# Route weights of a mixture of experts: from matmul spreading to DMA copies out of one partition each

## The reference, cut to what matters

```
probs = softmax(flat @ router_w.T)                 # 8 experts
tp, ti = top_k(probs, 2);  tp = tp / (sum(tp) + 1e-9)
weights = sum(tp[..., None] * one_hot(ti, 8), axis=1)
for e in range(8):
    hh = silu(flat @ w1[e].T) * (flat @ w3[e].T)   # 170 hidden features
    out = out + weights[:, e:e + 1] * (hh @ w2[e].T)
return layernorm(h + x + out)
```

## Time and profile before

| | |
|---|---|
| median of 3 runs | 124.4 us (123.87 to 124.7) |
| the profiled execution, its own time | 124.77 us |
| its span in the profile | 122.6 us |
| PE, DVE, ACT, POOL busy | 90%, 69%, 51%, 17% |
| granted TensorE clock over the span | 0.996 |

### The profile page before, as it was taken

How to read it: one execution, slowest core, us unless ns; L and a number is a source line. 1 busy time by engine, 2 the same in 40 slices (tenths; PEclk the granted TensorE clock), 3 DMA queues, 4 the chain that set the end, 5 groups by cost and what they waited for, 6 DMA issues and landing times.

```text
span 122.6 us, 2299 instructions
## 1 busy us (share of the span) xinstructions
PE 110.0 (90%) x890; PEld 72.7 (59%) x890; DVE 84.3 (69%) x181; ACT 62.8 (51%) x123; POOL 20.7 (17%) x46
## 2 busy tenths in 40 slices
PE   5978988899999999999599999799999999999920
PEld 2335537377776764877287888577888866232510
DVE  0001416697999597569887763469689997998981
ACT  4004466865332257635686348567476656247340
POOL 7400035000000000000013002154002340048400
PEclk9999999999999999999999999999999999999998
DMA  4999980000000000000000000000000000000003
GB/s 143 392 391 429 421 360 19 0 0 0 5 0 0 0 8 0 3 0 5 0 0 0 0 5 0 0 5 0 0 0 0 0 0 3 0 0 5 0 0 86
DMA packets 2682, 6.99 MB, mean 57 GB/s; under 512 B 1264, under 2 KB 1392, under 8 KB 2544
## 3 DMA queue, kind: packets, MB, share of 16 engines
q1 hardware_dynamic: 2128, 6.72, 13.9%
q10 hardware_dynamic: 544, 0.13, 0.5%
HBM read 6.59 MB, written 0.26 MB: 56 GB/s over the span
## 4 chain that ended last, share of the span: by engine, by line
PE 59%; DVE 19%; ACT 6%; DMA 5%; issue 4%; POOL 2%; SPq 1%; ACTq 0%; DVEq 0%
PE PS L649 7%; PE PS L650 7%; DMA shared_x<-x_dram 5%; PE PS L657 4%; PE PS L318 3%; PE PS L328 3%; PE PS L534 3%; PE PS L520 3%; PE PS L382 3%; DVE top L1137 2%; DVE shifted L1139 2%; PE PS L392 2%; PE PS L357 2%; PE PS L368 2%; PE PS L293 2%
## 5 line engine op out<-in xcount | busy, mean ns | idle before, releaser
L649 PE MATMUL PS<-xf,up_hi 128*128 128x512 f32 x44 | 17.8, 404 | 0.0
L650 PE MATMUL PS<-xf,up_lo 128*128 128x512 f32 x44 | 17.3, 394 | 0.0
L1331 DVE TENSOR_TENSOR shared_h<-PS,shared_f 128x512 f32<-128x512 f32 x22 | 14.9, 683 | 2.7 <-ACT shared_f L909 2.2
L909 ACT ACTIVATE shared_f<-PS 128x512 f32<-128x512 f32 x22 | 13.0, 596 | 6.3 <-PE PS L650 6.3
L1137 DVE TENSOR_REDUCE top<-PS 128x8 f32<-128x512 f32 x12 | 8.3, 688 | 3.7 <-PE PS L357 1.8
L649 PEld LDWEIGHTS PS<-xf,up_hi 128*128 128x128 f32 x44 | 8.3, 188 | 2.2 <-DVE shared_h L1331 0.2
L737 ACT ACT_TABLE_LOAD x7 | 9.0, 1283 | 0.8 <-PEq L1546 0.7
L650 PEld LDWEIGHTS PS<-xf,up_lo 128*128 128x128 f32 x44 | 8.3, 188 | 1.8
L989 POOL TENSOR_TENSOR qf<-shared_f 128x256 f32<-128x256 f32 x2 | 1.5, 728 | 44.1 <-DVE shared_f L1266 44.1
L808 ACT ACTIVATE probs<-PS 128x512 f32<-128x512 f32 x8 | 4.8, 597 | 7.9 <-PE PS L368 7.8
L285 PE MATMUL PS<-idle_bf 128*128 128x512 bf16 (+1 forms) x22 | 7.5, 446 | 1.3 <-POOL idle_bf L946 1.3
(11 more groups left out here) (194 smaller groups left out, 212.6 us busy)
## 6 DMA issues: line engine op xcount, KB each, us to landing
shared_x<-x_dram SPq DMA_DIRECT2D x3, 576.0 KB, 4.3
shared_x<-x_dram SPq DMA_DIRECT2D x3, 512.0 KB, 8.1
up_w<-pack_d_dram SPq DMA_DIRECT2D x1, 1408.0 KB, 12.4
pack_c_sb<-pack_c_dram SPq DMA_DIRECT2D x1, 796.5 KB, 13.2
pack_b_sb<-pack_b_dram SPq DMA_DIRECT2D x1, 455.0 KB, 9.4
down_w<-pack_e_dram SPq DMA_DIRECT2D x1, 352.0 KB, 13.5
pack_a_sb<-pack_a_dram SPq DMA_DIRECT2D x1, 162.0 KB, 6.6
out_dram<-normed SPq DMA_DIRECT2D x2, 64.0 KB, 1.8
```

Of the source, the lines that this page charges most:

```text
L649: mm(up, up_hi[:, at:at + P], moving, start=True, stop=False)
L650: mm(up, up_lo[:, at:at + P], moving, start=False, stop=True).then_inc(sem("up_mm"), 1)
L909: f(gate[:, n % UPBUF, :], PS[:, UP_BANKS[n % UPBUF][0], :], ACT.Silu).then_inc(sem("gated"), 1)
L1331: v.tensor_tensor(hh[:, ch, :, g * HC:(g + 1) * HC], PS[:, UP_BANKS[n % UPBUF][1], :].rearrange("q (s c) -> q s c", s=2), gate[:, n % UPBU ...
```

## The change: what it does

- The fourth of the four copies of the route weights is no longer split: it holds the full fp32 weights, and after PE's turn they are rows 96 to 111 of the PSUM bank (`EXACT_AT` = 96). A new ACT copy takes these 16 rows to a new tile, `route_exact`, ahead of the spread copies.
- SP waits for it and then issues 16 DMAs inside SBUF, each of which repeats one row of `route_exact` (2 KB in one partition) over 64 or 42 partitions: both streams of expert 2, of expert 3, the rests t = 4 and 5 (two experts each), then both streams of experts 4 to 7. Row `96 + 8 s + e` is the source for stream s and expert e.
- PE spreads experts 0 and 1 and rests 0 to 3 only. Six `spread_routes`, two `spread_rests` and six ACT copies go. The order of the down products is then free of spreading.
- POOL, not DVE, multiplies rests 4 and 5 into `hh`, SBUF by SBUF, before its four sums.
- Several semaphores of earlier stages are merged under one name with counts; their order is the same.

```diff
+        route_exact = sb("route_exact", [P, COLS])
+        rest_spread = (shared_f[:, UPBUF * COLS:(UPBUF + 1) * COLS], shared_x[:, (NE + 3) * COLS:(NE + 4) * COLS])
+        def spread_of(e):
+            return up_w[:, e * COLS:(e + 1) * COLS] if e < 5 else shared_x[:, (NE + e - 5) * COLS:(NE + e - 4) * COLS]
...
# SP
+            sp.wait_ge(sem("exact_made"), 1)
+            def send_route(s, e, dst, name):
+                line = EXACT_AT + s * NE + e
+                sp.dma_start(dst, route_exact[line:line + 1, :].unsqueeze(1).to_broadcast([1, dst.shape[0], COLS])).then_inc(sem(name), 16)
+            def send_expert(e):
+                for s in range(2):
+                    send_route(s, e, spread_of(e)[HALF * s:HALF * s + HALF], f"route_sent{min(e, 4 + e // 6 * 2)}")
+            def send_rests(t):
+                for n, e in enumerate(experts_of(t // 2)):
+                    send_route(t % 2, e, rest_spread[t - 4][n * REST:(n + 1) * REST], "rests_sent")
+            send_expert(2)
+            send_expert(3)
+            send_rests(4)
+            send_rests(5)
+            for e in range(4, NE):
+                send_expert(e)
...
# PE
-            spread_rests(3, 3)
+            spread_rests(3, 0)
+            pe.wait_ge(sem("exact_made"), 1)
             expert_down(1, DOWN_BANKS[1], every)
             pe.wait_ge(sem("rest_weighted"), 1)
             expert_down(2, DOWN_BANKS[2], every)
...
+            pe.wait_ge(sem("rest_weighted"), 2)
+            expert_down(3, DOWN_BANKS[3], every)
+            for e in range(4, NE):
+                pe.wait_ge(sem("expert_weighted"), e - 3)
+                expert_down(e, DOWN_BANKS[e], every)
             pe.wait_ge(sem("rest_weighted"), 4)
...
+            pe.wait_ge(sem("last_rests"), 2)
             rests_down(0)
...
# ACT
-            for e in range(NE):
+            f(route_exact[EXACT_AT:EXACT_AT + 2 * NE, :], PS[EXACT_AT:EXACT_AT + 2 * NE, ROUTED_BANK, :], ACT.Copy).then_inc(sem("exact_made"), 1)
+            for e in range(2):
...
# POOL
+            for t in (4, 5):
+                used = REST * len(experts_of(t // 2))
+                pool.wait_ge(sem("rests_sent"), 64)
+                g_.tensor_tensor(hh[0:used, t // 2, t % 2, :], hh[0:used, t // 2, t % 2, :], rest_spread[t - 4][0:used], ALU.mult)\
+                    .then_inc(sem("last_rests"), 1)
...
# DVE
-                ve.wait_ge(sem("routes_out"), e + 1)
+                if e < 2:
+                    ve.wait_ge(sem("routes_out"), e + 1)
+                else:
+                    ve.wait_ge(sem(f"route_sent{min(e, 4 + e // 6 * 2)}"), 32 if e < 4 else 64)
...
-                if e == 1:
-                    weight_rest(4)
-                    weight_rest(5)
```

More of the change, by code:

```diff
@@ L238, in build @@
         DOWN_BANKS = (4, 7, 1, 3, 4, 7, 1, 3)
-        REST_SPREAD_BANKS = (1, 3, 2, 6, 2, 6)
+        REST_SPREAD_BANKS = (1, 3, 2, 6)
+        EXACT_AT = 6 * 2 * NE
         LOGITS_BANK = 4
         ROUTED_BANK = 7
-        SPREAD_BANKS = (0, 5, 0, 5, 2, 6, 2, 6)
+        SPREAD_BANKS = (0, 5)
         FINAL_BANKS = (0, 5)
@@ L670, in spread_routes @@
             def spread_routes(e):
-                rows = slice(4 * NE * (e % 4), 4 * NE * (e % 4 + 1))
+                rows = slice(4 * NE * (e % 3), 4 * NE * (e % 3 + 1))
                 mm(PS[:, SPREAD_BANKS[e], :], pick[rows, e, :], route_rows[rows, :], start=True, stop=True)\
@@ L771, in _ @@
             act.wait_ge(sem("ffn1_down"), 1)
-            f(half(f1, 0), PS[:, FFN1_BANKS[0], 0:HC], ACT.Identity, bias=b("ff2_b")).then_inc(sem("f1_ready0"), 1)
+            f(half(f1, 0), PS[:, FFN1_BANKS[0], 0:HC], ACT.Identity, bias=b("ff2_b")).then_inc(sem("f1_ready"), 1)
             def queries1(g):
@@ L800, in _ @@
             act.wait_ge(sem("ffn1_down"), 2)
-            f(half(f1, 1), PS[:, FFN1_BANKS[1], 0:HC], ACT.Identity, bias=b("ff2_b")).then_inc(sem("f1_ready1"), 1)
+            f(half(f1, 1), PS[:, FFN1_BANKS[1], 0:HC], ACT.Identity, bias=b("ff2_b")).then_inc(sem("f1_ready"), 1)
             scale1 = float(HD) ** -0.5
@@ L1027, in _ @@
             pool.wait_ge(helped, 6)
-            four = routes.unsqueeze(2).to_broadcast([P, 4, 4, 2 * NE])
-            g_.tensor_copy(route_parts[:, :, :, 0, :].bitcast(F32R), four).then_inc(helped, 1)
+            three = routes.unsqueeze(2).to_broadcast([P, 4, 3, 2 * NE])
+            g_.tensor_copy(route_parts[:, :, 0:3, 0, :].bitcast(F32R), three).then_inc(helped, 1)
+            g_.tensor_copy(route_parts[:, :, 3, :, :], routes.unsqueeze(2).to_broadcast([P, 4, 2, 2 * NE])).then_inc(sem("route_split"), 1)
             pool.wait_ge(helped, 7)
-            g_.tensor_tensor(route_parts[:, :, :, 1, :], four, route_parts[:, :, :, 0, :], ALU.subtract).then_inc(sem("route_split"), 1)
+            g_.tensor_tensor(route_parts[:, :, 0:3, 1, :], three, route_parts[:, :, 0:3, 0, :], ALU.subtract).then_inc(sem("route_split"), 1)
+            for t in (4, 5):
[3 more added lines that the diff above has]
+                    .then_inc(sem("last_rests"), 1)
             def sum_pair(dst, other):
@@ L1050, in block_sums @@
             def block_sums(name, w, n):
-                v.reduce_sum(means[:, 0:n], w.rearrange("q (n d) -> q n d", d=D), AX).then_inc(sem(name + "_sum"), 1)
+                v.reduce_sum(means[:, 0:n], w.rearrange("q (n d) -> q n d", d=D), AX).then_inc(sem("block_sums"), 1)
             def less_means(name, w, n):
                 blocks = w.rearrange("q (n d) -> q n d", d=D)
-                ve.wait_ge(sem(name + "_sum"), 1)
+                ve.wait_ge(sem("block_sums"), 1 + ("av", "abv", "down").index(name))
                 return v.scalar_tensor_tensor(out=blocks, in0=means[:, 0:n].unsqueeze(2).to_broadcast([P, n, D]),
@@ L1404, in _ @@
                 ve.wait_ge(sem("down_mm"), e + 1)
-                ve.wait_ge(sem("routes_out"), e + 1)
-                v.tensor_tensor(product[:, e], PS[:, DOWN_BANKS[e], :], spread_w[:, e % 4], ALU.mult)\
+                if e < 2:
+                    ve.wait_ge(sem("routes_out"), e + 1)
+                else:
+                    ve.wait_ge(sem(f"route_sent{min(e, 4 + e // 6 * 2)}"), 32 if e < 4 else 64)
+                v.tensor_tensor(product[:, e], PS[:, DOWN_BANKS[e], :], spread_of(e), ALU.mult)\
                     .then_inc(sem("expert_weighted"), 1)
-                if e == 1:
-                    weight_rest(4)
-                    weight_rest(5)
                 if e == 5:
```

80 lines of the change are left out of this document (28 added, 52 removed).

## The result

The changed kernel takes 155.45 us (median of 4 runs, 155.33 to 156.72) against 124.33: a ratio of 1.2503, 95% interval 1.2459 to 1.2548, 31.1 us slower. The forecast was 160 us, its own range 150 to 189. The profiled execution has a span of 153.5 us and an own time of 155.33.

The account below looks back on a forecast made before the run. PE and DVE, both nearly full, then a chain of short steps bounded the kernel. Last landing 148.2, plus 9.05 tail, 0.4 clock and 2.17 between span and own time: 160 us; own range 150 to 189, over all cases 125 to 190.

Parts of the forecast that it names:

- The source's rate: SP's transfers inside SBUF: one source partition gives 26.8 GB/s, so a 64-row transfer takes 4.89 us, a 42-row one 3.21.
- Who is served side by side: SP's transfers: six expert pairs side by side, 29.3 us, and the rests' transfers singly, 12.8 us; sum 42.2 us.
- Who waits: POOL, PE's rest products and DVE wait for transfers; only the last landing, at 148.2 us, counts.
- The tail and the clock: After the last landing: 9.05 us of tail, plus 0.4 if PE's clock falls and the turning of the total doubles.
- The splitting on POOL: Three route-weight copies split in place of four, one copied plain: 0, between -0.2 and +0.2 us.
- the moved spread copies: ACT's two spread copies move by 0.6 us behind the exact copy, to about 105.3; hidden.
- the new PE wait: PE's wait for the exact copy, before the down product of expert 1; hidden.
- The signs: Expected in the changed profile: landings of ten us and more, DVE waits, 27 to 54 GB/s, POOL idle until about 128.
- C (between): Rival on the transfers: one source gives two to eight times 26.8 GB/s; 139 us at 54 GB/s, 128 at 107; chance 12%.
- B (faster): Rival: sources at full rate, with quicker issue and landing than the rows say; 123.3 us at best; chance 11%.
- A's condition: Rival: a row read above about 290 GB/s, SP's issue sets the pace, POOL becomes the bound; 126.1 us; chance 15%.
- DVE alone would gain 1.5 us: DVE, spared two rest products with nothing else in the way, reaches its last sum at 114.1, not 115.62.

Follow-up runs that it names:

- experiments 1: The changed kernel with all sixteen DMAs reading the same row, partition 96; 187.04 us (one execution).
- experiment 4: Three edits of the changed kernel: transfers read partitions 96 to 99 only, 96 and 64 in turn, or 96 and 100 in turn; 187.15, 187.06, 155.94 us.
- experiment 2: The changed kernel with each of the sixteen DMAs reading as many SBUF partitions as it writes; 129.15 us, ratio 1.0396.
- experiment 3: The changed kernel with each of the sixteen DMAs repeating a 2 KB row of the up weights from HBM; 129.06 us, ratio 1.0362.
- experiment 6: The changed kernel with as many source partitions as targets and 8 DMAs in place of 16, same bytes; 126.76 us, ratio 1.0171.
- experiment 7: The kernel before, with POOL weighting rests 4 and 5 from ACT's copies, no DMA; two forms with different PE spreading order; 124.50 and 124.67 us.

## Why the prediction was right, step by step

| step | predicted | measured |
|---|---|---|
| exact copy ends, SP starts | 104.2 | 103.8 |
| expert 2 / expert 3 used | 115.8 / 115.8 | 114.3 / 117.5 |
| POOL starts the rests | 128.6 | 124.9 |
| expert 4 used | 138.4 | 136.1 |
| expert 6 used | 148.2 | 144.2 |
| from there to the end of the span | 9.05 + 0.4 | 9.3 |
| own time | 160 | 155.3 |

**The source's rate.** Right, and its size too: 26.8 GB/s taken as a sixteenth of the fastest slice, 27 measured (experiments 1 and 4). That working had luck in it. I divided by the sixteen engines and called the result the pace of one partition; what the experiments show is the pace of a group of partitions, with all engines at work, and no run here says why the two come to the same number. The 8.9 GB/s bound drawn from a matmul's stream had no bearing on DMA.

**Who is served side by side.** This is the term that was mis-sized, and its 3.6 us are most of the 4.5 between forecast and measurement; SP's earlier start (0.4) and a smaller difference between span and own time (1.83 in place of 2.17) make most of the rest. I took 42.2 us, with the expert pairs at twice 26.8 and the rests' transfers, twos from neighbours, singly at 12.8 us. From the issue of the first, with 1.8 us for landing, to the last use it was 144.18 - 103.77 - 1.8 = 38.6 us. From the use of expert 3 to the rests it took 7.5 us, not 12.8: the stretches there move 48 and 53 GB/s, not 27, so a rest of one group must have run beside a transfer of another. The first experts ran slower than at twice the rate: 13.7 us from SP's start to the use of expert 3, where the estimate had 11.6, and 11.2 for experts 4 and 5 in place of 9.8. Experts 6 and 7 then took 8.1, less than 9.8, so that the last eight transfers together took 19.3 us, where the estimate had 19.6. The delay of the first four goes with the slow start, 20 to 26 GB/s up to 108 us. The mean of 50 GB/s is just under two groups: the sources of experts 2 and 3 alternate between the groups of 96 and 104, those of experts 4 to 7 between the groups of 100 and 108, and the kernel of experiment 4 that has two groups only took the same time, 155.94 us.

**Who waits.** Right: POOL idled 24.53 us before its rests, and PE's rest products came late and slowly (5.2 us for 24 where it was 2.8), but both were off the path; only the last landing counted. The loss is DVE's idle time before products 2, 3, 4 and 6, less the work that it was spared. I had left out the one before 3, since I let both pairs land together.

**The tail and the clock.** PE was busy for 2.49 of 5 us from 107, then for 1.92, and its granted clock went from 1.00 to 0.74 and 0.50 (the two levels are 2.4 and 1.2 GHz). After five us with PE busy throughout, from 137, it was back at 1.00 from 142, and at 0.51 in the tail. There the turning of the total took 1.12 us where it was 0.77. The tail grew by 9.3 - 9.05 = 0.27 us, near the 0.4 foreseen.

**The splitting on POOL, the moved spread copies, the new PE wait**: no cost to be seen. The splitting took 1.15 us, from 99.23 to 100.38, where it was 1.22, and DVE's first product follows its rests without a pause, as before.

**The signs.** DVE's waits and POOL's idle time came as announced, and the slices nearly (up to 59 GB/s, where I had said 54). What stands ahead of the stage ran as before, 0.4 us earlier in this profile. The median time to landing of the 64-row transfers did not: 9.3 and 8.9 us, where I had said ten and more. It also includes the time behind other transfers, so it is no measure of one transfer's pace.

**The rivals.** C (between) and B (faster) did not happen. A's condition, that the sources are read at full rate, was never met by this kernel, but experiments 2, 3 and 6 came near it. Its sign was right and its size too small: 129.15 and 129.06 against 126.1. Its mechanism, POOL as the bound, held in experiment 6 only, with 8 issues. In experiment 2 DVE came to its last sum after POOL was done (119.50): the weights of experts 4 and 5 were used at 114.04, not at 110.95, because issues of 0.60 to 0.90 us and a landing of 2.3 add up, and the two sums took 3.44 us against the 2.25 that I had for them. So even without the crowded source the change did not pay in any form that was run, and B's hope, issues of 0.26 us, was far off.

**What was wrong in the reading of before.** That DVE alone would gain 1.5 us if relieved: experiment 7 took 1.27 us off DVE and the time did not move. I had read the pauses of DVE only; PE's down products stood right behind. And SP's issue was taken from its shortest rows; the same trace has one of 0.52 and one of 1.10 us (of `pack_c` and `pack_d`), and copies inside SBUF took 0.60 to 0.90. The sum of the transfers all in twos is 35.8 us, not 34.9, which makes the low end 153 us where I had 152; the range of 150 to 189 stands.

## What to carry to other kernels

A DMA that repeats one SBUF row was limited here by the way out of that row's group of partitions, about 27 GB/s, with all 16 DMA engines busy. For such a DMA, divide its bytes by that before anything else. Then spread the sources over groups, or read the row from HBM, or let a matmul with a 0/1 matrix do it (a pair of these took 0.50 us in the kernel before). DMA engines that were busy for 80% at an eighth of their bandwidth, with issues that lasted microseconds, were held up by the data and not by the issuer; to tell the two apart, change the source and leave the issues alone, as experiments 1 and 2 do. And before work is moved off a full engine, ask of each engine beside it whether it is full as well: in this stage PE was as full as DVE, and relief of DVE alone gave nothing. Relief of PE alone was not tried.

## What the runs showed of the hardware

- Groups of source partitions: 96 with 97 to 99, and 96 with 64, share 27 GB/s; 96 and 100 give 50 together (187.15, 187.06, 155.94 us, one execution each).
- One HBM row repeated to 64 partitions showed no such limit, up to the 195 GB/s of experiment 3: 3.0 us from issue to landing, against 8.9 to 9.3 out of SBUF in the changed kernel.
- POOL and DVE: a DVE sum of two SBUF operands took 0.69 us when POOL was idle and 1.6 to 1.8 beside POOL's operations on SBUF (changed kernel against experiments 2 and 6); DVE products that read PSUM and SBUF kept their 0.64. The Trainium skill says on "SBUF — State Buffer", section "Who interferes with whom", that such a sum and a GpSimd operation that reads SBUF shut each other out for whole instructions. By that rule, the trace agrees: in experiment 6 the two sums were longer by 0.91 and 1.10 us, when some 1.05 and 1.25 us were left of the operation that POOL had just begun, and POOL's next operation took 1.72 us in place of 1.27.
- Two queues with the same sources, targets and bytes moved 86 GB/s where one moved 61.
- In the first 4 us of the transfers no kernel with repeated SBUF rows moved more than 27 GB/s, whatever the number of groups and queues.
